# Mamba-2 mixer layer: the carried state's part is added to the diagonal product in PSUM, C times each head's growth on GpSimd, and a new order of the unit

## The chip, the cores and the metric

The kernel runs on one core of one Trainium2 chip. The metric is the device time of one execution in microseconds (us), the median of several runs. A profiled execution is one such run with the hardware profiler on; its "span" goes from the first to the last instruction.

## What is computed

The reference is a layer norm, a Mamba-2 (state space) mixer with a residual, a second layer norm, and a dense layer with a low-rank mixture added, with a residual. Nearly all of the work is the mixer. Sizes: batch 2, sequence 512 in 4 chunks of 128, hidden 512, 128 heads of 64, state 128, 8 groups of 16 heads that share B and C.

```python
L = jnp.exp(_segsum(A_dt))
Y_diag = jnp.einsum('bzlhn,bzshn,bhzls,bzshp->bzlhp', Cc, Bc, L, xch)
states = jnp.einsum('bzlhn,bhzl,bzlhp->bzhpn', Bc, decay_states, xch)
...
Y_off = jnp.einsum('bzlhn,bzhpn,bhzl->bzlhp', Cc, prev, jnp.exp(A_cum))
Y = (Y_diag + Y_off).reshape(b, s, H, P) + hs * D[None, None, :, None]
g = y * jax.nn.silu(gate)
```

`Y_diag` is the part inside a chunk, `Y_off` what the state of the earlier chunks brings, multiplied by `exp(A_cum)`, here called a head's growth. Then follow a norm over each group of 1024 channels and the output projection.

## The kernel before

The instructions of every engine are written out by hand, with semaphores between the engines; nothing is scheduled by a compiler. `mixer` walks over 8 groups (`g`) of 8 units (`j`, running number `k`). A unit is 128 channels, two heads (`PAIR`), for both batches (`b`). Products of weights are made of three products of a high and a low part in fp32r, each with 512 moving columns (I call these the large matmuls); the small ones are fp32 with 128 columns, and each such matmul shows as two records in the profile. In a unit TensorE does:

- `project` (L708) of the next unit's x into `x_bank` and of its gate into `g_bank`, 12 large matmuls for each batch, 48 in all; in units 4 and 5 also the next group's B and C (24 more);
- `out_product` (L766) for four 128-token blocks, 24 large matmuls, c = 0, 1 into `x_bank`, c = 2, 3 into `d_bank`;
- `states` (L718), `diagonal` (L726, into `d_bank`), `carry` (L735) and `turn_hs` (L742, transposes), the small ones. One bank, `turn_bank`, takes the transposes of both batches in turn, and one, `state_bank`, the states and the carried product of both batches in turn, so the four steps for a batch are spread between the large ones.

VectorE reads x out of PSUM with three taps of the convolution (`tap`, L1072), multiplies the transposed x by dt (`to_heads`, L1143), the decay matrix by B·C (`score`, L1098), carries the state over the chunks (`carried_state`, L1106), and makes y in three steps: `carry_part` (L1123) multiplies the carried product in `state_bank` by the growth, `skip` (L1130) adds D·x to the diagonal product, `add_carry` (L1136) adds the two. `y_low_part` (L1092) makes y's low part, `add_outs` (L1160) adds output blocks into `acc`, and `normed_out` (L1171) adds the last group's 8 finished blocks, scaled, into `mixed`: 2, 3 and 3 of them in units 1, 2 and 3 of each group after the first. In units 5 and 6 VectorE has three taps more, for B and C (`bc_tap`, L1082). ScalarE makes the exponentials (`decays`), the silus, y's high part and its square (`finish`), and the weights' high parts (`high_part`). GpSimd multiplies y by the gate (`gated`, L1319), dt·x by the decay (`decayed`, L1325), sums squares (`add_squares`, L1312) and makes low parts of weights (`low_part`, L1306, and L1343). SyncE issues all loads in one queue; `load_grown` (L622) copies each head's growth to 64 partitions.

## Time and profile before

| what | value |
|---|---|
| runs (3) | median 1673.87 us, 1670.74 to 1675.4 |
| the profiled execution | 1673.45 us, span 1671.7 us |
| mean granted clock of TensorE | 0.989 of full speed |
| DMA | 164.56 MB, mean 98 GB/s |

The busy shares of the engines are in the first rows of the section below. A unit is best read as the distance from its first `d_bank` matmul (L731) to the next unit's.

### The profile page before, as it was taken

Reading aid. Unit: us, or ns where it says so; the run is one execution under the profiler, and the core shown is the slowest. Engines: PE = TensorE matmul, PEld = TensorE weight load, DVE = VectorE, ACT = ScalarE, POOL = GpSimd, SP = SyncE. Lnnn points to the kernel's source line nnn. Section 1 sums busy time; section 2 is a strip of 40 time slices with the busy share of each in tenths; the row PEclk is TensorE's granted clock in tenths of the full one; section 3 lists DMA queues with packets and bytes.
Section 4 is the critical chain, followed back from the end, with each engine's and each line's share of the span. In section 5 each row is a group of like instructions: output and inputs, shape, how many; then the busy total and the mean of one; then the engine's idle time right before and its main releaser. Section 6 shows DMA issues by size and latency. Waiting matters only on the chain.

```text
span 1671.7 us, 26883 instructions
## 1 busy us (share of the span) xinstructions
PE 1620.5 (97%) x9616; PEld 1343.2 (80%) x9616; DVE 1361.8 (81%) x1974; ACT 1140.1 (68%) x2002; POOL 838.9 (50%) x543
## 2 busy tenths in 40 slices
PE   7779999999999999999999999999999999999987
PEld 4568888888888888888888888888888888888866
DVE  7567787997889788897879978897888978799756
ACT  5577667776787677766677767776777666877721
POOL 1145545564455545465445644565454654556542
PEclk9989999999999999999999999999999999999988
DMA  5423232323232332332223232323323232233111
GB/s 200 178 96 112 80 109 88 109 83 107 97 98 90 104 102 80 111 97 87 101 91 107 93 107 86 105 82 107 102 76 112 101 97 87 96 101 108 58 41 51
DMA packets 88244, 164.56 MB, mean 98 GB/s; under 512 B 23344, under 2 KB 39728, under 8 KB 87856
## 3 DMA queue, kind: packets, MB, share of 16 engines
q1 hardware_dynamic: 88112, 162.85, 30.0%
q8 instruction: 77, 1.26, 0.3%
q14 instruction: 55, 0.45, 0.1%
HBM read 157.03 MB, written 5.77 MB: 97 GB/s over the span
## 4 chain that ended last, share of the span: by engine, by line
PE 77%; issue 7%; POOL 6%; DVE 5%; ACT 1%; DVEq 0%; POOLq 0%; ACTq 0%
PE g_bank L713 7%; PE g_bank L715 7%; PE g_bank L714 7%; PE x_bank L713 6%; PE x_bank L715 6%; PE d_bank L731 6%; PE x_bank L714 6%; PE state_bank L738 5%; PE state_bank L722 5%; PE turn_bank L745 3%; PE x_bank L772 3%; PE x_bank L770 3%; PE x_bank L771 3%; PE d_bank L772 3%; PE d_bank L770 3%
## 5 line engine op out<-in xcount | busy, mean ns | idle before, releaser
L1323 POOL TENSOR_TENSOR y<-y,gate 128x512 f32<-128x512 f32 x128 | 223.4, 1745 | 457.5 <-DVE y L1140 457.5
L1078 DVE SCALAR_TENSOR_TENSOR hs<-x_bank,cols,hs 128x1022 f32<-128x1022 f32 (+2 forms) x192 | 244.6, 1274 | 85.1 <-ACT hs L940 82.8
L930 ACT ACTIVATE scores<-scores,tables 128x128 f32<-128x128 f32 x1024 | 312.4, 390 | 1.1 <-DMA scores<-sums_dram 1.1
L713 PE MATMUL g_bank<-x_high,w_high 128*128 128x512 f32 x624 | 258.0, 413 | 1.2 <-DVE bc L1156 1.2
L1330 POOL TENSOR_TENSOR xdecay<-xdt,tables 128x384 f32<-128x384 f32 x128 | 146.1, 1141 | 200.6 <-DVE xdt L1150 200.6
L715 PE MATMUL g_bank<-x_high,w_low 128*128 128x512 f32 x624 | 245.6, 394 | 0.0
L714 PE MATMUL g_bank<-x_low,w_high 128*128 128x512 f32 x624 | 243.9, 391 | 0.0
L1309 POOL TENSOR_TENSOR w_low<-raw,w_high 128x512 fp32r<-128x512 f32 x141 | 192.5, 1374 | 91.0 <-ACT w_high L920 91.0
L713 PE MATMUL x_bank<-x_high,w_high 128*128 128x512 f32 x512 | 213.8, 418 | 0.5 <-PEq L146 0.5
L715 PE MATMUL x_bank<-x_high,w_low 128*128 128x512 f32 x512 | 202.0, 395 | 0.0
L714 PE MATMUL x_bank<-x_low,w_high 128*128 128x512 f32 x512 | 200.9, 392 | 0.0
L952 ACT ACTIVATE hs<-hs 128x1024 f32<-128x1024 f32 x64 | 67.9, 1060 | 185.2 <-DVE hs L1078 185.1
L1103 DVE TENSOR_TENSOR scores<-scores,bc 128x1024 f32<-128x1024 f32 x128 | 178.2, 1401 | 8.2 <-ACT scores L933 7.9
L1317 POOL TENSOR_TENSOR square_sum<-square_sum,gate 128x1024 f32<-128x1024 f32 x56 | 167.9, 2998 | 2.2 <-ACT gate L981 2.2
L1169 DVE TENSOR_TENSOR acc<-d_bank,acc 128x512 f32<-128x512 f32 x96 | 65.4, 689 | 99.9 <-PE d_bank L772 99.9
L715 PEld LDWEIGHTS g_bank<-x_high,w_low 128*128 128x128 f32 x624 | 117.5, 188 | 27.3
L933 ACT ACTIVATE scores<-scores 128x1024 f32<-128x1024 f32 x128 | 135.9, 1062 | 2.8
L714 PEld LDWEIGHTS g_bank<-x_low,w_high 128*128 128x128 f32 x624 | 118.2, 189 | 21.2
L713 PEld LDWEIGHTS g_bank<-x_high,w_high 128*128 128x128 f32 x624 | 118.1, 189 | 21.4 <-DVE bc L1156 1.5
L731 PEld LDWEIGHTS d_bank<-scores,xdt 128*64 128x64 f32 x2048 | 110.5, 137 | 24.2 <-issue 22.2
L1117 DVE SCALAR_TENSOR_TENSOR state<-state,chunk_tab,state_bank 128x64 f32<-128x64 f32 x512 | 121.1, 278 | 9.1
L731 PE MATMUL d_bank<-scores,xdt 128*64 128x128 f32 x2048 | 126.2, 276 | 1.7 <-DVE xdt L1150 1.7
(172 smaller groups left out, 3602.6 us busy)
## 6 DMA issues: line engine op xcount, KB each, us to landing
scores<-sums_dram SPq DMA_DIRECT2D x128, 512.0 KB, 4.9
raw<-w_in SPq DMA_DIRECT2D x144, 256.0 KB, 3.0
grown_rows<-grown_dram SPq DMA_DIRECT2D x256, 96.0 KB, 2.7
out_raw<-w_out SPq DMA_DIRECT2D x64, 256.0 KB, 3.2
xt<-x SPq DMA_DIRECT2D x8, 256.0 KB, 5.3
mixed<-x SPq DMA_DIRECT2D x1, 2048.0 KB, 11.7
out<-mixed SPq DMA_DIRECT2D x8, 256.0 KB, 2.0
table_dram<-table SPq DMA_DIRECT2D x2, 768.0 KB, 3.2
```

The costliest lines, as they stand in the source:

```text
L713: pe.matmul(to, w_high[:, slot, k], x_high[:, b, k], start=(k == 0), stop=False)
L714: pe.matmul(to, w_high[:, slot, k], x_low[:, b, k], start=False, stop=False)
L715: mm = pe.matmul(to, w_low[:, slot, k], x_high[:, b, k], start=False, stop=(k == KT - 1))
L731: mm = pe.matmul(d_bank[r * HEAD_DIM:(r + 1) * HEAD_DIM, b, c * P:(c + 1) * P], xdt[:, b, c, r], scores[:, s, b, r, c], start=True, stop=True)
L930: op = s.activation(at, at, ACT.Relu, bias=col[:, r, c:c + 1], scale=-1.0)
L933: s.activation(scores[:, q % 2, b], scores[:, q % 2, b], ACT.Exp, scale=-1.0).then_inc(exp_ready, 1)
L1078: v.scalar_tensor_tensor(out=hs[:, q % 2, :, i:], in0=x_bank[:, :, 0:SEQ - i], scalar=cols[:, q, TAPS - 1 - i:TAPS - i], in1=hs[:, q % 2, ...
L1103: v.tensor_tensor(at, at, bc[:, b].rearrange("p c l -> p (c l)").unsqueeze(1) .to_broadcast([P, PAIR, SEQ]), ALU.mult).then_inc(scores_rea ...
L1309: pool.tensor_tensor(w_low[:, slot], raw[:, slot], w_high[:, slot].bitcast(F32), ALU.subtract)\
L1317: pool.tensor_tensor(square_sum[:], square_sum[:], gate[:, q % 2], ALU.add).then_inc(square_added, 1)
L1323: pool.tensor_tensor(y[:, b], y[:, b], gate[:, q % 2, b], ALU.mult).then_inc(y_ready, 1)
L1330: pool.tensor_tensor(xdecay[:, b], xdt[:, b, 0:LATER], col.unsqueeze(3).to_broadcast([P, LATER, PAIR, HEAD_DIM]), ALU.mult)\
```

## The change

- `carry` no longer writes the bare product into `state_bank`. It multiplies by C times growth, which differs by head, so it is two matmuls of 64 output partitions where there was one of 128, and it accumulates on the diagonal product in `d_bank`. Only `skip` is left to make y, now for each batch.
- `grown_of` on GpSimd multiplies `grown_c` by C in place, 128x768 for each batch. `load_grown` copies both heads' growth to all 128 partitions, twice the bytes, and waits for `carried`.
- Each batch has its own bank (`head_bank`) for transposes and states.
- TensorE's unit is now: outputs c = 2, 3 of the unit before, x for both batches, states and diagonal of both, gate for both, outputs c = 0, 1, (B or C of the next group), carry of both, transposes of both. There are two stretches of 36 large matmuls.
- VectorE, ScalarE and GpSimd are reordered to match.

```diff
     x_bank, g_bank, d_bank, turn_bank, state_bank = banks
     out_bank = [x_bank[:, 0], x_bank[:, 1], d_bank[:, 0], d_bank[:, 1]]
+    head_bank = [turn_bank, state_bank]
...
-        grown = sb("grown_rows", [P, BATCH, LATER, P])
+        grown_c = sb("grown_c", [P, BATCH, PAIR, LATER, P])
...
             def load_grown(k, b):
-                reached(sp, y_sum, BATCH * (k - 1) + b + 1)
+                reached(sp, carried, BATCH * (k - 1) + b + 1)
                 rows = grown_dram[b * ALL + k].rearrange("(r n) -> r n", r=PAIR)
-                for r in range(PAIR):
-                    sp.dma_start(grown[r * HEAD_DIM:(r + 1) * HEAD_DIM, b].rearrange("p c l -> p (c l)"),
-                                 rows[r, P:].partition_broadcast(HEAD_DIM)).then_inc(grown_in[b], 16)
+                sp.dma_start(grown_c[:, b].rearrange("p r c l -> p r (c l)"), rows[:, P:].partition_broadcast(P))\
+                  .then_inc(grown_in[b], 16)
...
                 for c in range(CHUNKS):
                     for r in range(PAIR):
                         mm = pe.matmul(d_bank[r * HEAD_DIM:(r + 1) * HEAD_DIM, b, c * P:(c + 1) * P],
-                                       xdt[:, b, c, r], scores[:, s, b, r, c], start=True, stop=True)
+                                       xdt[:, b, c, r], scores[:, s, b, r, c], start=(c == 0), stop=False)
                 mm.then_inc(diag_done, 1)
...
             def carry(k, b):
+
                 pe.wait_ge(state_ready, BATCH * k + b + 1)
+                pe.wait_ge(grown_c_ready, BATCH * k + b + 1)
                 for c in range(LATER):
-                    mm = pe.matmul(state_bank[:, c * P:(c + 1) * P], state[:, b, c].rearrange("p r d -> p (r d)"),
-                                   c_feat[:, b, (c + 1) * P:(c + 2) * P], start=True, stop=True)
+                    for r in range(PAIR):
+                        mm = pe.matmul(d_bank[r * HEAD_DIM:(r + 1) * HEAD_DIM, b, (c + 1) * P:(c + 2) * P],
+                                       state[:, b, c, r], grown_c[:, b, r, c], start=False, stop=(c == LATER - 1))
                 mm.then_inc(carried, 1)
 
             def turn_hs(k, s, b):
                 pe.wait_ge(hs_ready, k + 1)
+                reached(pe, state_ready, BATCH * (k - 1) + b + 1)
                 for c in range(CHUNKS):
-                    mm = pe.transpose(turn_bank[:, c * P:(c + 1) * P], hs[:, s, b, c * P:(c + 1) * P], ident[:])
+                    mm = pe.transpose(head_bank[b][:, c * P:(c + 1) * P], hs[:, s, b, c * P:(c + 1) * P], ident[:])
                 mm.then_inc(turned, 1)
...
+            def later_outs(j, k):
+
+                for c in (2, 3):
+                    if k < ALL:
+                        pe.wait_ge(y_sum, BATCH * k + c - 1)
+                    else:
+                        pe.wait_ge(added, emptied(k - 1, c))
+                    out_product(j, c)
...
+                    if k > 2:
+                        later_outs(j - 1, k - 1)
+                    if k == ALL + 1:
+                        pe.wait_ge(square_added, (UNITS - 1) * GROUPS)
+                        var_of()
                     if ahead:
                         pe.wait_ge(conv_ready, k + 1)
-                        reached(pe, added, emptied(k - 1, 0))
-                        project(ahead[0], x_at, 0, x_bank[:, 0])
+                        for b in range(BATCH):
+                            reached(pe, added, emptied(k - 1, b))
+                            project(ahead[0], x_at, b, x_bank[:, b])
...
+                            pe.wait_ge(b_tok_ready, g + 1)
+                        for b in range(BATCH):
+                            states(k, b)
                         for b in range(BATCH):
                             reached(pe, added, emptied(k - 1, 2 + b))
                             diagonal(k, s, b)
...
+                        for b in range(BATCH):
+                            project(ahead[0], x_at + 1, b, g_bank[:, b])
+                    if k > 1:
                         pe.wait_ge(y_low_ready, k - j % 2)
                         pe.wait_ge(out_low_ready, k - j % 2)
...
+                    if j in (4, 5) and not last:
+                        pe.wait_ge(gate_ready, BATCH * (k + 2))
+                        for b in range(BATCH):
+                            project(g, (NEXT_B, NEXT_C)[j - 4], b, g_bank[:, b])
+                    if now:
+                        for b in range(BATCH):
+                            carry(k, b)
                     if ahead:
...
+                        for b in range(BATCH):
+                            turn_hs(k + 1, (j + 1) % 2, b)
+                    if j == 0 and g > 0:
+                        pe.wait_ge(square_added, (UNITS - 1) * g)
+                        pe.wait_ge(gate_ready, BATCH * (k + 2))
+                        var_of()
...
                     if ahead:
-                        decays(k + 1, ahead[0], ahead[1], 1)
                         tap0(*ahead)
...
                     if ahead:
+                        decays(k + 1, ahead[0], ahead[1], 0)
                         silu_hs(k + 1, (j + 1) % 2)
...
-                    if second:
-                        decays(k + 2, second[0], second[1], 0)
+                    if ahead:
+                        decays(k + 1, ahead[0], ahead[1], 1)
+                    if j == UNITS:
+                        group_std(GROUPS)
...
-            def skip(q, k):
-                v.wait_ge(diag_done, BATCH * (k + 1))
+            def skip(q, k, b):
+                v.wait_ge(carried, BATCH * k + b + 1)
                 reached(v, squared, k)
-                v.scalar_tensor_tensor(out=y[:], in0=hs[:, q % 2], scalar=d_col[:, q:q + 1], in1=d_bank[:],
-                                       op0=ALU.mult, op1=ALU.add).then_inc(skip_added, 1)
+                v.scalar_tensor_tensor(out=y[:, b], in0=hs[:, q % 2, b], scalar=d_col[:, q:q + 1], in1=d_bank[:, b],
+                                       op0=ALU.mult, op1=ALU.add).then_inc(y_sum, 1)
...
-                    turn_over, takes_bc = j == UNITS - 1 and not last, j in (5, 6) and not last
-                    early = isinstance(g, int) and g == 0
-                    flush = not (early and j < 2)
-
-                    to_heads(g, j, k, 1)
-                    if turn_over:
-                        keep_bc(g + 1)
-                    if takes_bc:
+
+                    for b in range(BATCH):
+                        to_heads(g, j, k, b)
+                    if k > 2:
+                        add_outs(g, j - 1, (2,))
+                    if j in (5, 6) and not last:
                         for i in range(1, TAPS):
                             bc_tap(i, 2 * (g + 1) + j - 5, j - 5)
-                        carried_state(*now, 0)
-                    elif ahead:
-                        score(ahead[0], ahead[1], k + 1, 0)
+                    for b in range(BATCH):
+                        score(g, j, k, b)
+                    if k > 2:
+                        add_outs(g, j - 1, (3,))
+                    if j == UNITS - 1 and not last:
+                        keep_bc(g + 1)
                     if prev:
                         y_low_part(prev[1], prev[2])
-                    if not takes_bc:
-                        carried_state(*now, 0)
-                    if not early:
+                    if j == 1 and g > 0:
+                        group_rstd(g)
+                    if g > 0:
                         for at in {1: (0, 1), 2: (2, 3, 4), 3: (5, 6, 7)}.get(j, ()):
                             normed_out(g, at)
                     if ahead:
-                        tap(1, *ahead)
-                    carry_part(k, 0)
-                    if ahead:
-                        tap(2, *ahead)
-                        tap(3, *ahead)
-                    carried_state(*now, 1)
-                    skip(j, k)
-                    add_carry(k, 0)
-                    if takes_bc:
-                        score(ahead[0], ahead[1], k + 1, 0)
-                    if ahead:
-                        score(ahead[0], ahead[1], k + 1, 1)
-                    carry_part(k, 1)
-                    add_carry(k, 1)
-                    if flush:
+                        for i in range(1, TAPS):
+                            tap(i, *ahead)
+                    for b in range(BATCH):
+                        carried_state(*now, b)
+                    for b in range(BATCH):
+                        skip(j, k, b)
+                    if k > 1:
                         add_outs(g, j, (0, 1))
-                    if ahead:
-                        to_heads(ahead[0], ahead[1], k + 1, 0)
-                    if flush:
-                        add_outs(g, j, (2, 3))
-                    if j == 0 and not early:
-                        group_rstd(g)
...
+            def grown_of(q, k, b):
+                if q == 0:
+                    pool.wait_ge(c_ready, k // UNITS + 1)
+                pool.wait_ge(grown_in[b], 16 * (k + 1))
+                at = grown_c[:, b].rearrange("p r c l -> p r (c l)")
+                pool.tensor_tensor(at, at, c_feat[:, b, P:].unsqueeze(1).to_broadcast([P, PAIR, LATER * P]), ALU.mult)\
+                    .then_inc(grown_c_ready, 1)
+
             def body(g, last):
                 for j in range(UNITS):
                     k = UNITS * g + j
-                    prev, ahead = unit(g, last, j - 1), unit(g, last, j + 1)
+                    prev = unit(g, last, j - 1)
                     splits = splits_of(g, last, j)
-                    decayed(j, k, 1)
-                    if prev:
-                        add_squares(*prev)
+                    for b in range(BATCH):
+                        decayed(j, k, b)
+                    for at in splits[:1]:
+                        low_part(*at)
                     pool.wait_ge(out_high_ready, k + 1)
                     pool.tensor_tensor(out_low[:, j % RING], out_raw[:, j % 2], out_high[:, j % RING].bitcast(F32),
                                        ALU.subtract).then_inc(out_low_ready, 1)
-                    for at in splits[:2]:
+                    if prev:
+                        add_squares(*prev)
+                    for b in range(BATCH):
+                        grown_of(j, k, b)
+                    for at in splits[1:]:
                         low_part(*at)
-                    gated(j, k, 0)
-                    gated(j, k, 1)
-                    if ahead:
-                        decayed(ahead[1], k + 1, 0)
-                    for at in splits[2:]:
-                        low_part(*at)
+                    for b in range(BATCH):
+                        gated(j, k, b)
```

The same in the order of instructions. VectorE, third unit of a group (j = 2), before, from its one `score` to `skip`:

```order
L1103 TENSOR_TENSOR scores<-scores,bc 128x1024
L1094 SCALAR_TENSOR_TENSOR y_low<-y,cols,y_high 128x1024
L1112 COPY state<-state_bank 128x128
L1117 SCALAR_TENSOR_TENSOR state<-state,chunk_tab,state_bank 128x64 x4
L1173 SCALAR_TENSOR_TENSOR mixed<-acc,g_rstd,mixed 128x512 x3
L1078 SCALAR_TENSOR_TENSOR hs<-x_bank,cols,hs 128x2x511
L1128 TENSOR_TENSOR grown_rows<-state_bank,grown_rows 128x384
L1078 SCALAR_TENSOR_TENSOR hs<-x_bank,cols,hs 128x2x510
L1078 SCALAR_TENSOR_TENSOR hs<-x_bank,cols,hs 128x2x509
L1112 COPY state<-state_bank 128x128
L1117 SCALAR_TENSOR_TENSOR state<-state,chunk_tab,state_bank 128x64 x4
L1133 SCALAR_TENSOR_TENSOR y<-hs,cols,d_bank 128x1024
```

and now, from the `to_heads` of both batches:

```order
L1128 TENSOR_TENSOR xdt<-turn_bank,tables 128x512
L1128 TENSOR_TENSOR xdt<-state_bank,tables 128x512
L1148 TENSOR_TENSOR acc<-d_bank,acc 128x512
L1095 TENSOR_TENSOR scores<-scores,bc 128x1024 x2
L1148 TENSOR_TENSOR acc<-d_bank,acc 128x512
L1086 SCALAR_TENSOR_TENSOR y_low<-y,cols,y_high 128x1024
L1152 SCALAR_TENSOR_TENSOR mixed<-acc,g_rstd,mixed 128x512 x3
L1070 SCALAR_TENSOR_TENSOR hs<-x_bank,cols,hs 128x2x511
L1070 SCALAR_TENSOR_TENSOR hs<-x_bank,cols,hs 128x2x510
L1070 SCALAR_TENSOR_TENSOR hs<-x_bank,cols,hs 128x2x509
L1104 COPY state<-turn_bank 128x128
```

Both scores, y_low and the three `normed_out` (`mixed`) now follow each other ahead of the taps (`hs`); before, one score stood here and the other behind `skip`.

GpSimd, the same unit, before, from `decayed`:

```order
L1330 TENSOR_TENSOR xdecay<-xdt,tables 128x384 x2
L1317 TENSOR_TENSOR square_sum<-square_sum,gate 128x1024
L1343 TENSOR_TENSOR out_low<-out_raw,out_high 128x512
L1309 TENSOR_TENSOR w_low<-raw,w_high 128x512 x2
L1323 TENSOR_TENSOR y<-y,gate 128x512 x2
```

and now:

```order
L1294 TENSOR_TENSOR xdecay<-xdt,tables 128x384 x2
L1273 TENSOR_TENSOR w_low<-raw,w_high 128x512
L1316 TENSOR_TENSOR out_low<-out_raw,out_high 128x512
L1281 TENSOR_TENSOR square_sum<-square_sum,gate 128x1024
L1303 TENSOR_TENSOR grown_c<-grown_c,c_feat 128x768 x2
L1273 TENSOR_TENSOR w_low<-raw,w_high 128x512
L1287 TENSOR_TENSOR y<-y,gate 128x512 x2
```

The square sum and the two new products with C stand between the low part of the output weights and the second low part.

VectorE, sixth unit (j = 5), before, behind the taps for B, the first batch's state and the taps:

```order
L1112 COPY state<-state_bank 128x128
L1117 SCALAR_TENSOR_TENSOR state<-state,chunk_tab,state_bank 128x64 x4
L1133 SCALAR_TENSOR_TENSOR y<-hs,cols,d_bank 128x1024
L1140 TENSOR_TENSOR y<-y,grown_rows 128x384
L1103 TENSOR_TENSOR scores<-scores,bc 128x1024 x2
```

and now, from `to_heads` on:

```order
L1128 TENSOR_TENSOR xdt<-turn_bank,tables 128x512
L1128 TENSOR_TENSOR xdt<-state_bank,tables 128x512
L1148 TENSOR_TENSOR acc<-d_bank,acc 128x512
L1079 SCALAR_TENSOR_TENSOR bc_conv<-g_bank,tap_bc,bc_conv 128x2x511
L1079 SCALAR_TENSOR_TENSOR bc_conv<-g_bank,tap_bc,bc_conv 128x2x510
L1079 SCALAR_TENSOR_TENSOR bc_conv<-g_bank,tap_bc,bc_conv 128x2x509
L1095 TENSOR_TENSOR scores<-scores,bc 128x1024 x2
L1148 TENSOR_TENSOR acc<-d_bank,acc 128x512
L1086 SCALAR_TENSOR_TENSOR y_low<-y,cols,y_high 128x1024
```

The scores are now those of the same unit, and stand behind the three taps for B (`bc_conv`).

## Rows read from the trace of the kernel before

**Rows 1.** The page: busy time by engine.
```profile
PE 1620.5 (97%) x9616; PEld 1343.2 (80%) x9616; DVE 1361.8 (81%) x1974; ACT 1140.1 (68%) x2002; POOL 838.9 (50%) x543
```

**Rows 2.** Busy time in stretches, columns in the first line: two middle units, one longer, two first.
```profile
core 0: us, PE busy (x) PEld busy (x) DVE busy (x) ACT busy (x) POOL busy (x), PEclk, DMA share, GB/s
886.45:908.71 22.26, 22.26 (x137) 18.62 (x137) 20.38 (x30) 16.27 (x29) 11.12 (x8) 1.00 0.31 101
908.71:931.48 22.77, 22.70 (x137) 18.47 (x136) 22.40 (x31) 16.26 (x29) 14.53 (x9) 1.00 0.29 99
954.25:981.95 27.70, 27.70 (x161) 23.13 (x161) 18.86 (x29) 18.10 (x31) 14.42 (x11) 1.00 0.28 91
...
81.24:110.91 29.67, 21.35 (x114) 17.01 (x113) 19.39 (x31) 25.61 (x51) 13.90 (x10) 0.83 0.27 85
110.91:131.96 21.05, 18.39 (x114) 15.40 (x113) 15.39 (x23) 16.25 (x29) 11.85 (x8) 0.92 0.30 101
```

**Rows 3.** Timeline of TensorE, start and duration in us: a unit; 36 large matmuls.
```profile
886.45 1.97 PE L731 MATMUL d_bank<-scores,xdt 128*64 128x128 f32 x32
888.35 0.94 PE L738 MATMUL state_bank<-c_feat,state 128*128 128x128 f32 x6
889.04 0.47 PE L713 MATMUL g_bank<-x_high,w_high 128*128 128x512 f32 x1
...
891.89 0.83 PE L722 MATMUL state_bank<-xdecay,b_tok 128*128 128x128 f32 x6
...
966.93 0.48 PE L713 MATMUL g_bank<-x_high,w_high 128*128 128x512 f32 x1
...
975.21 0.60 PE L745 MATMUL turn_bank<-ident,hs 128*128 128x128 f32 x4
```

**Rows 4.** Page, costliest groups: busy us, mean ns of one, idle before.
```profile
L1140 DVE TENSOR_TENSOR y<-y,grown_rows 128x384 f32<-128x384 f32 x128 | 97.2, 759 | 8.9
L920 ACT ACTIVATE w_high<-raw 128x512 fp32r<-128x512 f32 x141 | 87.2, 618 | 10.4 <-PEq L146 10.4
L976 ACT ACTIVATE y_high<-y,cols 128x1024 fp32r<-128x1024 f32 x64 | 73.2, 1144 | 20.8 <-POOL y L1323 20.8
L1128 DVE TENSOR_TENSOR grown_rows<-state_bank,grown_rows 128x384 f32<-128x384 f32 x128 | 70.6, 551 | 7.7 <-PE state_bank L738 6.8
```

**Rows 5.** Timeline of VectorE, five places.
```profile
809.86 3.90 DVE L1087 SCALAR_TENSOR_TENSOR bc_conv<-g_bank,tap_bc,bc_conv 128x1022 f32<-128x1022 f32 x3
...
829.01 1.28 DVE L1169 TENSOR_TENSOR acc<-x_bank,acc 128x512 f32<-128x512 f32 x2
...
834.69 2.36 DVE L1103 TENSOR_TENSOR scores<-scores,bc 128x1024 f32<-128x1024 f32 x1
...
907.50 5.07 DVE L1173 SCALAR_TENSOR_TENSOR mixed<-acc,g_rstd,mixed 128x512 f32<-128x512 f32 x3
...
919.72 1.22 DVE L1103 TENSOR_TENSOR scores<-scores,bc 128x1024 f32<-128x1024 f32 x1
...
1628.69 2.73 DVE L1173 SCALAR_TENSOR_TENSOR mixed<-acc,g_rstd,mixed 128x512 f32<-128x512 f32 x4
```

**Rows 6.** Timeline of GpSimd, two places.
```profile
832.77 0.84 POOL L1330 TENSOR_TENSOR xdecay<-xdt,tables 128x384 f32<-128x384 f32 x1 [0.95 <-DVE xdt L1150]
833.57 2.40 POOL L1317 TENSOR_TENSOR square_sum<-square_sum,gate 128x1024 f32<-128x1024 f32 x1
838.26 1.30 POOL L1343 TENSOR_TENSOR out_low<-out_raw,out_high 128x512 fp32r<-128x512 f32 x1 [2.29 <-ACT out_high L1010]
...
905.25 3.39 POOL L1317 TENSOR_TENSOR square_sum<-square_sum,gate 128x1024 f32<-128x1024 f32 x1
908.61 1.73 POOL L1343 TENSOR_TENSOR out_low<-out_raw,out_high 128x512 fp32r<-128x512 f32 x1
```

**Rows 7.** Timeline of TensorE: a wait at the start, one at the end.
```profile
102.56 0.72 PE L745 MATMUL turn_bank<-ident,hs 128*128 128x128 f32 x4 [3.76 <-DVE xdt L1150]
...
1616.18 3.57 PE L762 MATMUL turn_bank<-mean_col,square_sum 128*128 128x2 f32 x16 [4.17 <-POOL square_sum L1317]
```

156 lines of the change are left out of this document (47 added, 109 removed).

## Prediction

> **What bounds the kernel now.** I read the page first: TensorE is busy for 97% of the span, VectorE 81%, ScalarE 68%, GpSimd 50% [rows 1]. A share over the span could hide waits, so I then read the busy time in stretches from one unit's first `d_bank` matmul to the next [rows 2]. A middle unit takes 22.26 us, all of it TensorE's; a third or fourth unit of a group 22.77, where VectorE is busy for 22.40; a unit with B's or C's projection 27.70. The first two take 29.67 and 21.05 us with 21.35 and 18.39 busy. So TensorE's queue is the bound, and a change can gain by making the same matmuls denser or by removing waits at the two ends. It can lose only if an operand comes late on TensorE, and the engine with least spare time is VectorE.
>
> The sum is made against the profiled execution, 1673.45 us; its span of 1671.7 leaves 1.75 us around it, and the median of the runs is 0.42 us above it, so no correction is needed.
>
> **The change, part by part.**
>
> *Matmuls, per unit.* The large ones are the same 72. Twelve between small ones take 2.85 us (889.04 to 891.89), 36 in one stretch 8.28 (966.93 to 975.21) [rows 3]. Six times 2.85 is 17.1, twice 8.28 is 16.6: 0.5 us less. The new carry is 12 fp32 matmuls of 64 output partitions, 24 records. The diagonal has exactly this form, 32 records in 1.90 us (886.45 to 888.35), so 24 take about 1.45. The old carry is 6 records in 0.69 behind the diagonal [rows 3], and a little less elsewhere, 1.3 for both. That is +0.15, and changing between 64 and 128 output partitions once more adds up to 0.2. Net between -0.35 and +0.05 us per unit; I take -0.1, times 64: **-6 us** (-22 to +3).
>
> *Waits that go.* A third or fourth unit has 0.51 us over the plain one [rows 2], and I allow 0.5 more per group for the turn-over units: 1.5 x 7 = **-11 us**.
>
> *The start.* Units without an output product should take 22.26 - 2 x 2.85 = 16.6 us; the first two take 50.7 together [rows 2], 17.5 over. The waits come from handing one bank from batch to batch, as the 3.76 us of the second transposes for VectorE's xdt [rows 7], and the granted clock is 0.83 and 0.92 there [rows 2]. With a bank per batch I still find 3.5 us (second batch's exponential, first carried state): **-13 us** (-8 to -17).
>
> *The end.* The last output blocks now run while the last y is gated and split, 2.7 us of work in what was idle, and the variance (waiting 4.17 us for the square sum [rows 7]) comes behind an output product: **-4 us** (-1 to -6).
>
> *VectorE's work.* The two 384-column operations per batch go: the addition alone is 0.76 us each [rows 4]. This is costed at nothing, since its spare time is not TensorE's; the cover is TensorE's 22 us per unit. *Growth loads* double to 384 KB per batch, some 25 MB over the run; the DMA share is 0.31 [rows 2], so they too are hidden: the product with C needs them over 10 us after they are issued.
>
> *GpSimd's new products.* 384 columns take 0.84 us alone, 1024 take 2.40, 512 take 1.30 [rows 6]; 768 lie between, 1.8. Twice per unit, 3.6 us. GpSimd is busy for 11 to 14.5 of 22 us [rows 2], so its queue holds that. What it costs is VectorE's time. A VectorE operation that has two SBUF inputs waits for a GpSimd operation that is running: the score at 834.69 ended 1.08 us after the square sum that began at 833.57 (+2.40), taking 2.36 instead of 1.22; three `normed_out` took 5.07 us beside GpSimd, while four took 2.73 without it [rows 5, 6]. That is 1.69 each: GpSimd's 1.3 for a 512-column operation and 0.4 of its own. The two take turns, an operation each. So beside GpSimd each such operation costs the whole of whatever GpSimd has in its queue there.
>
> The Trainium skill says the same as a rule ("SBUF — State Buffer", Who interferes with whom): the later of the two fully blocks until the first finishes. By that rule an operation of 2.3 us blocks for 2.3; if instead a block never exceeded the 1.3 us that this trace shows, the sum would be the first rival's. The turns in rows 5 and 6 agree with the rule, for operations up to 1.3 us.
>
> *Third and fourth unit.* I lay the new order out in time from T, the start of a unit's first stretch. TensorE: 8.3 outputs and x, 3.2 states and diagonal, 5.5 gates, so at **T+17.0** it needs the taps (`out_product` into `x_bank`). VectorE: `skip` may start when the first carry ends, T-1.1; two skips, two adds, two xdt and one add at about 0.62 (1.28 for two [rows 5]) bring it to T+3.2. GpSimd: gates y until T+2.2, then ScalarE makes y's high part (1.14), the square of like length and two copies of 0.62 [rows 4], so GpSimd's row of work starts at T+5.5 and has no gap: low part, output weight's low part, square sum 2.3, 1.8, 1.8. VectorE in turns with it: scores end T+6.0 (0.6 blocked by xdecay), add 6.6, y_low 8.3, first `normed_out` 10.0 (behind the output weight), second 12.7 (behind the square sum), third 15.1 (behind the first product with C); three taps of 3.7 (three such take 3.90 [rows 5]) end at **T+18.9**. TensorE waits 2.0 us. With two `normed_out` (second unit) the taps end by T+17, without any by T+13.5: no wait. Two units, 7 groups: **+28 us**.
>
> *Sixth and seventh unit.* Three taps for B or C stand ahead of the scores, T+3.2 to 7.0. First score: behind the output weight's low part, 9.0. Second: behind the square sum, 12.4; the add that frees `d_bank` 13.0. TensorE wants the second diagonal at T+10.6 and gets it at 13.1, 2.5 us late. Two units, 7 groups: **+35 us**.
>
> Sum: 1673.45 - 6 - 11 - 13 - 4 + 28 + 35 = 1702.5, say **1702 us**. This case's own range is 1685 to 1722.
>
> **The rivals.**
> 1. *Faster: the new waits hardly appear.* If a block costs 1.15 us at most, the taps end at T+17.1 and the second diagonal is 1.3 late: 14 x 1.3 = 18, 1658 us. It also comes out so if GpSimd's row of work starts a few tenths later than I have it, since the first score of the sixth unit misses its turn by 0.3 us only; with no waits at all it is 1640. For it: VectorE loses 1.5 us per unit and more of work. Against: the whole-operation turns of rows 5 and 6.
> 2. *About the same: one of the two places waits, not both.* 1639.5 + 28 = 1667.5 or + 35 = 1674.5.
> 3. *Slower still: the clock.* The second unit has a granted clock of 0.92 over 21.05 us [rows 2]: some 3.4 us at 1.2 instead of 2.4 GHz, 1.7 us lost, behind a wait like the 3.76 us one [rows 7]. If each of 28 waits of 2 us or more did that, +1.7 x 28 = 48: 1750 us. Against it: a group's steady waits here are 0.5 us, so no row shows what 2 us do.
> 4. *The carry is not paired* in the two halves of the output partitions as the diagonal is: 24 records at 0.11 us, +1.3 per unit, 1785 us. The identical form of L731 speaks against it.
>
> **How the numbers follow.** Forecast 0.48, first rival 0.30, second 0.12, third 0.08, fourth 0.02. A measurement tells 0.3% (5 us) from no change. Faster: the first rival, 0.30. Same: most of the second, 0.10. Slower: the rest, 0.60. For eight in ten the range starts inside the first rival, where 18 us of waits and a larger gain at the start still fit, 1645, and ends above the forecast's own range, 1725; the third and fourth rival and the lowest part of the first stay out.
>
> **What would show it.** Right: units three and four at about 24 us, six and seven with 2.5 us of idle TensorE before the diagonal, ended by VectorE's add or score; scores and `normed_out` well over 1.2 and 0.74 us, taking turns with square sum and `grown_c`; a plain unit at 22.1 to 22.3; the first `d_bank` matmul of the third unit some 13 us earlier; carry records like the diagonal's. Wrong: all middle units at about 22.2, or a wait for GpSimd's `grown_c` before the carry, which I place at T+17 against a need at T+19.7.

## The result, and where the 34 microseconds came from

The changed kernel takes **1707.76 us** (median of four runs, 1706.11 to 1709.0) where the kernel before takes 1674.36 (1670.74 to 1675.4): a ratio of 1.020, interval 1.0186 to 1.0214. Forecast were 1702 and "slower", with a range of 1645 to 1725. The profiled span went from 1671.7 to 1707.3 us.

The page of the kernel after, busy time by engine and then the granted clock in 40 slices:

```profile
PE 1622.7 (95%) x10384; PEld 1348.9 (79%) x10384; DVE 1282.8 (75%) x1782; ACT 1151.1 (67%) x2002; POOL 1036.5 (61%) x671
...
PEclk9899999999999999999999999999999999999999
```

Against [rows 1] VectorE has lost 79 us of busy time, though part of what is left is blocking, GpSimd has gained 198, and TensorE's busy time is 2.2 us more with 768 records more. The span is 35.6 us longer, so nearly all of that is time in which TensorE waits. Where it does, the stretches from one first diagonal to the next show. Kernel after, a second, a third, a fourth and a sixth unit of one group, then the first two units of the run:

```profile
core 0: us, PE busy (x) PEld busy (x) DVE busy (x) ACT busy (x) POOL busy (x), PEclk, DMA share, GB/s
905.24:927.53 22.29, 22.29 (x150) 18.70 (x149) 18.21 (x27) 17.54 (x31) 12.64 (x10) 1.00 0.40 119
927.53:951.51 23.98, 22.57 (x150) 18.62 (x149) 22.19 (x29) 16.20 (x30) 16.63 (x11) 1.00 0.36 110
951.51:975.45 23.94, 22.54 (x150) 18.62 (x149) 20.51 (x27) 16.30 (x31) 16.61 (x11) 1.00 0.36 111
1003.18:1033.19 30.01, 27.98 (x174) 23.18 (x173) 22.29 (x28) 18.92 (x33) 18.10 (x12) 1.00 0.36 100
...
84.74:104.07 19.33, 17.37 (x125) 14.18 (x125) 13.86 (x21) 19.21 (x35) 12.51 (x9) 1.00 0.49 144
104.07:120.93 16.86, 16.86 (x125) 14.19 (x125) 14.00 (x20) 16.77 (x30) 14.22 (x10) 1.00 0.52 157
```

Beside [rows 2]: the plain unit has hardly moved (22.26 to 22.29), the third is 23.98 instead of 22.77, the fourth 23.94, a unit with B's or C's work up to 30.0 instead of 27.70, and the first two take 36.2 instead of 50.7. The waits of TensorE name the two places. Kernel after; waiter, releaser, us in total, times, longest:

```profile
PE d_bank L732 <- DVE acc L1148: 29.0, 15, 2.0
PE x_bank L775 <- DVE hs L1070: 19.6, 14, 1.4
```

The first is the second batch's diagonal in the sixth and seventh unit of seven groups, released by the add that VectorE does behind the second score. The second is the first output product in the third and fourth unit, waiting for the taps. Each also costs 0.2 to 0.3 us of restart, so the distances grow by 2.25 and 1.67 us.

The fourth unit of that group, as VectorE (first block) and GpSimd (second) saw it, T = 941.81; start and duration in us. The third unit has the same durations to 0.01 us:

```profile
944.74 2.88 DVE L1095 TENSOR_TENSOR scores<-scores,bc 128x1024 f32<-128x1024 f32 x2
...
948.14 1.70 DVE L1086 SCALAR_TENSOR_TENSOR y_low<-y,cols,y_high 128x1024 fp32r<-128x1024 f32 x1
949.76 6.80 DVE L1152 SCALAR_TENSOR_TENSOR mixed<-acc,g_rstd,mixed 128x512 f32<-128x512 f32 x3
956.49 3.90 DVE L1070 SCALAR_TENSOR_TENSOR hs<-x_bank,cols,hs 128x1022 f32<-128x1022 f32 x3
```
```profile
948.72 2.26 POOL L1316 TENSOR_TENSOR out_low<-out_raw,out_high 128x512 fp32r<-128x512 f32 x1
950.94 2.82 POOL L1281 TENSOR_TENSOR square_sum<-square_sum,gate 128x1024 f32<-128x1024 f32 x1
953.71 4.56 POOL L1303 TENSOR_TENSOR grown_c<-grown_c,c_feat 128x768 f32<-128x768 f32 x2
```

The three `normed_out` take 6.80 us (5.07 in [rows 5]) beside the square sum and the products with C; the taps end at T+18.6 (forecast T+18.9). And the seventh unit, VectorE and GpSimd; the sixth, 30.01 us earlier, has the same durations:

```profile
1026.42 3.90 DVE L1079 SCALAR_TENSOR_TENSOR bc_conv<-g_bank,tap_bc,bc_conv 128x1022 f32<-128x1022 f32 x3
1030.24 5.42 DVE L1095 TENSOR_TENSOR scores<-scores,bc 128x1024 f32<-128x1024 f32 x2
1035.58 0.68 DVE L1148 TENSOR_TENSOR acc<-d_bank,acc 128x512 f32<-128x512 f32 x1
```
```profile
1031.22 3.35 POOL L1281 TENSOR_TENSOR square_sum<-square_sum,gate 128x1024 f32<-128x1024 f32 x1
1034.53 5.60 POOL L1303 TENSOR_TENSOR grown_c<-grown_c,c_feat 128x768 f32<-128x768 f32 x2
```

They take turns: the first score waits for the output weight's low part, the square sum (2.40 us alone [rows 6], 3.35 here) for the first score, and the second score for the square sum: it ends at 1035.6, 1.1 us behind the square sum's end at 1034.6, so its own work of 1.22 us [rows 5] runs only there. One by one the two scores take 2.12 and 3.38 us: the low part holds the first for 0.9 us, the square sum the second for 2.2. In the kernel before, the square sum of such a unit ends 11 us before its scores begin. VectorE and GpSimd of the kernel before, sixth unit:

```profile
991.33 3.45 DVE L1103 TENSOR_TENSOR scores<-scores,bc 128x1024 f32<-128x1024 f32 x2
```
```profile
977.58 2.40 POOL L1317 TENSOR_TENSOR square_sum<-square_sum,gate 128x1024 f32<-128x1024 f32 x1
```

The account of the +35.6 us of span, from the distances of all 64 units: ahead of the first diagonal +3.5; first two units -14.5; the unit distances of the rest without their new waits -6.2 (last less first diagonal, less the first two units: 1460.7 us in the kernel both_moved below against 1466.9 before); taps late 23.4; second diagonal late 31.5; the clock of TensorE, below, 4.7; from the last diagonal to the end -6.8. The two ends are known less well than the middle: in the eight traces of the kernel after and of the variants below that leave no work out and keep TensorE's order, the first diagonal starts at 82.2 to 85.7 us and the stretch from the last one to the end takes 65.4 to 67.3. The kernel before has one trace, with 81.2 and 72.8.

### The profile page after: what moved, and what is told of

The parts are those of the page before. It is cut to its first block, busy times and chain, and to the rows that moved or that the text cites. A ratio compares the mean times of both kernels' runs of the same rounds, so it can differ in the third digit from the quotient of the medians.

```text
span 1707.3 us, 28048 instructions
## 1 busy us (share of the span) xinstructions
PE 1622.7 (95%) x10384; PEld 1348.9 (79%) x10384; DVE 1282.8 (75%) x1782; ACT 1151.1 (67%) x2002; POOL 1036.5 (61%) x671
## 4 chain that ended last, share of the span: by engine, by line
POOL 51%; issue 39%; PE 3%; ACT 2%; DVE 1%; POOLq 0%; DVEq 0%; ACTq 0%
POOL grown_c L1303 15%; POOL w_low L1273 10%; POOL square_sum L1281 7%; POOL y L1287 7%; POOL out_low L1316 7%; POOL xdecay L1294 6%; ACT scores L925 1%; DVE mixed L1152 0%; PE turn_bank L798 0%; PE turn_bank L800 0%; PE turn_bank L799 0%; PE g_bank L756 0%; PE state_bank L800 0%; PE state_bank L798 0%; PE state_bank L799 0%
## 5 line engine op out<-in xcount | busy, mean ns | idle before, releaser
L1287 POOL TENSOR_TENSOR y<-y,gate 128x512 f32<-128x512 f32 x128 | 162.5, 1292 | 391.4 <-DVE y L1118 391.3
L1118 DVE SCALAR_TENSOR_TENSOR y<-hs,cols,d_bank 128x512 f32<-128x512 f32 x128 | 90.2, 745 | 288.6 <-PE d_bank L742 288.6
L1303 POOL TENSOR_TENSOR grown_c<-grown_c,c_feat 128x768 f32<-128x768 f32 x128 | 279.8, 2207 | 0.0
L713 PE MATMUL g_bank<-x_high,w_high 128*128 128x512 f32 x624 | 252.9, 405 | 1.3 <-DVE bc L1135 1.3
L935 ACT ACTIVATE hs<-x_bank,cols 128x1024 f32<-128x1024 f32 x64 | 77.1, 1204 | 213.2 <-PE x_bank L715 156.4
L1095 DVE TENSOR_TENSOR scores<-scores,bc 128x1024 f32<-128x1024 f32 x128 | 212.6, 1699 | 7.3 <-ACT scores L928 7.1
L713 PE MATMUL x_bank<-x_high,w_high 128*128 128x512 f32 x512 | 199.5, 390 | 0.5 <-PEq L146 0.5
L1281 POOL TENSOR_TENSOR square_sum<-square_sum,gate 128x1024 f32<-128x1024 f32 x56 | 161.7, 2888 | 2.2 <-ACT gate L976 2.2
L732 PE MATMUL d_bank<-scores,xdt 128*64 128x128 f32 x2048 | 130.3, 278 | 30.7 <-DVE acc L1148 29.0
```

Of the source, the lines that this page charges most:

```text
L713: pe.matmul(to, w_high[:, slot, k], x_high[:, b, k], start=(k == 0), stop=False)
L732: mm = pe.matmul(d_bank[r * HEAD_DIM:(r + 1) * HEAD_DIM, b, c * P:(c + 1) * P], xdt[:, b, c, r], scores[:, s, b, r, c], start=(c == 0), st ...
L1095: v.tensor_tensor(at, at, bc[:, b].rearrange("p c l -> p (c l)").unsqueeze(1) .to_broadcast([P, PAIR, SEQ]), ALU.mult).then_inc(scores_rea ...
L1281: pool.tensor_tensor(square_sum[:], square_sum[:], gate[:, q % 2], ALU.add).then_inc(square_added, 1)
L1287: pool.tensor_tensor(y[:, b], y[:, b], gate[:, q % 2, b], ALU.mult).then_inc(y_ready, 1)
L1303: pool.tensor_tensor(at, at, c_feat[:, b, P:].unsqueeze(1).to_broadcast([P, PAIR, LATER * P]), ALU.mult)\
```

## The experiments

The expectations count units from 0, so their unit 2 is the third and their unit 5 the sixth; "A" is the theory of the prediction. Line numbers in the rows are of each run's own kernel, which differ by a few. The kernel before took 1674.6 to 1675.5 us (medians) beside these runs.

### Moving VectorE's two blocked pieces

```
# normed_late, VectorE: between y_low_part and the taps
-                    if g > 0:
-                        for at in {1: (0, 1), 2: (2, 3, 4), 3: (5, 6, 7)}.get(j, ()):
-                            normed_out(g, at)
# and put behind carried_state, ahead of skip; add_outs, where it overwrites acc:
                     if j % UNITS in (2, 3):
+                        reached(v, mixed_ready, TB * (g - 1) + CHUNKS * b + c + 1)
# scores_first: bc_tap(1..3) of j = 5, 6 now stand behind the two score(g, j, k, b)
# both_moved: both edits together
```

> The kernel after the change, with VectorE's two or three normed_out updates of units 1, 2 and 3 of a group moved from ahead of the taps to behind the carried states. Theory A (VectorE's updates whose inputs all lie in SBUF take turns with GpSimd's products, so that they stretch wherever GpSimd is busy): the three updates stood beside the square sum and the growth products at 6.80 us; behind the carried states GpSimd has run out of work, so they cost nearer 0.7 to 1.7 us each, and the taps end about 6 us earlier. TensorE's wait ahead of the first outs of units 2 and 3 (1.69 and 1.65 us, in seven groups, 23.4 us together) goes: 1684 us (1680 to 1689); the wait of the diagonal for the scores stays at about 29 us. Theory B (VectorE has too much work in these units, whatever stands beside it): the updates take their 6.8 us at the new place too and make the skip late: no gain, 1705 to 1715. Theory C (the growth transfers of double size are the cause): no change, 1707.

Measured **1684.1 us** (1680.09 to 1685.53). VectorE and GpSimd in the third unit:

```profile
912.56 3.91 DVE L1070 SCALAR_TENSOR_TENSOR hs<-x_bank,cols,hs 128x1022 f32<-128x1022 f32 x3 [1.67 <-ACT hs L935]
...
918.82 2.29 DVE L1153 SCALAR_TENSOR_TENSOR mixed<-acc,g_rstd,mixed 128x512 f32<-128x512 f32 x3
```
```profile
917.92 1.32 POOL L1274 TENSOR_TENSOR w_low<-raw,w_high 128x512 fp32r<-128x512 f32 x1
```

The same three updates take 2.29 us instead of 6.80 where GpSimd has one last low part left; third and fourth unit are 22.29 in all groups, and the diagonal's wait is 28.9 us, no different from the kernel after (29.0). That is what A expected; B and C, which expected no gain, fall here. The taps would be in time behind this move whether or not anything is blocked, since the updates no longer stand ahead of them; what speaks for the turns is the 2.29 us against 6.80.

> The kernel after the change, with the scores of units 5 and 6 put ahead of the three taps of B or C on VectorE. Theory A: the pair of scores then stands beside GpSimd's xdecay and low parts and no longer beside the square sum, and ends 4 us earlier; the diagonal's wait of 2.25 us in two units of seven groups (31.5 us) goes. The taps of B or C end near 12.3 us behind the start of the outs, where TensorE wants their bank at 11.6, and the taps of the next unit end up to 1 us late, so 0 to 1.2 us of each 2.25 come back: 1683 us (1676 to 1695). Theory B (VectorE's amount of work sets these two units): the wait only moves from the diagonal to the next bank, and the gain is under 5 us: 1703 to 1708. Theory C (double growth transfers): no change.

Measured **1673.33 us** (1670.02 to 1674.26). A's direction, and below its range: the whole 31.5 us goes without the small price that was expected, and in this trace the clock falls behind no unit of the steady part, which gives back the 4.7 us too. Sixth unit, VectorE:

```profile
974.49 2.88 DVE L1095 TENSOR_TENSOR scores<-scores,bc 128x1024 f32<-128x1024 f32 x2
977.29 3.90 DVE L1079 SCALAR_TENSOR_TENSOR bc_conv<-g_bank,tap_bc,bc_conv 128x1022 f32<-128x1022 f32 x3
...
981.70 1.49 DVE L1086 SCALAR_TENSOR_TENSOR y_low<-y,cols,y_high 128x1024 fp32r<-128x1024 f32 x1
```

The scores cost 2.88 for two instead of 5.42, the taps of B pass the square sum unhindered, and y_low comes to 1.49 instead of 2.24. VectorE starts the next taps 12.9 us behind its first skip instead of 16.2, so nothing is late.

> Both moves at once: normed_out behind the carried states, and the scores of units 5 and 6 ahead of the taps of B and C. Theory A: the two gains lie in different units and add: 1660 us (1652 to 1672), faster than the kernel before the change (1674). Theory B: no gain over the two alone, 1700 or more. Theory C: 1707.

Measured **1649.3 us** (1648.99 to 1649.86), ratio to before **0.984** (0.9827 to 0.986): 1.6% faster than the kernel before, 3.4% faster than the change. That is below A's range too, as the small price of scores_first did not come. It is what was forecast as the first rival's "no waits at all", 1640, but for 9 us. The gains of the two moves (24 and 34) add to 58. Page:

```profile
PE 1609.9 (98%) x10384; PEld 1346.0 (82%) x10384; DVE 1157.5 (70%) x1782; ACT 1152.5 (70%) x2002; POOL 990.7 (60%) x671
```

VectorE does the same 1782 instructions in 125 us less busy time than in the kernel after.

### GpSimd's side: length, order, and which product

```
# halved_ops, GpSimd
-                pool.tensor_tensor(square_sum[:], square_sum[:], gate[:, q % 2], ALU.add).then_inc(square_added, 1)
+                for b in range(BATCH):
+                    op = pool.tensor_tensor(square_sum[:, b], square_sum[:, b], gate[:, q % 2, b], ALU.add)
+                op.then_inc(square_added, 1)
# and grown_of: one tensor_tensor per head r on grown_c[:, b, r] instead of one for both
```

> The kernel after the change, with GpSimd's square sum cut in two halves of 512 columns and each growth product cut in two of 384, one per head; the work and its place in GpSimd's order are the same. Theory A in its strict form (an update of VectorE waits until the product that GpSimd has begun is through): each of VectorE's updates waits half as long, the two scores of units 5 and 6 take about 4.2 us instead of 5.42, the three normed_out about 5.2 instead of 6.80, and some 25 us come back: 1683 us (1675 to 1690). Rival D (the two engines share the port evenly while both are at work, whatever the length of an instruction): durations and time stay, 1705 to 1710, or rise by GpSimd's cost of three more instructions per unit.

Measured **1666.61 us** (1664.96 to 1668.88). VectorE and GpSimd, sixth unit:

```profile
971.67 4.32 DVE L1095 TENSOR_TENSOR scores<-scores,bc 128x1024 f32<-128x1024 f32 x2
```
```profile
972.64 4.48 POOL L1282 TENSOR_TENSOR square_sum<-square_sum,gate 128x512 f32<-128x512 f32 x2
```

The score pair takes 4.32 us, 4.2 expected, at the same work: a block lasts as long as the other engine's instruction, and sharing by halves (D) is refuted. The time fell by 41 us where 25 were expected, because a wait is a difference: the mean `normed_out` fell from 2.04 to 1.58 us, which is enough to bring the taps of the third and fourth unit in time (22.29 to 22.35), so 23.1 of those 23.4 us went; the diagonal's wait fell to 13.7 us in total, which takes 15 us off the distances; and behind the shorter waits the clock did not fall, another 4.7.

```
# growth_tiny: grown_of multiplies grown_c[:, b] [:, :, 0:1] by c_feat[:, b, P:P + 1] only
# squares_tiny: add_squares adds gate[:, q % 2, :, 0:1] to square_sum[:, :, 0:1] only
# both_tiny: both
# growth_late, GpSimd's body: all the work kept, order changed
-                    for b in range(BATCH):
-                        grown_of(j, k, b)
                     for at in splits[1:]:
                         low_part(*at)
+                    for b in range(BATCH):
+                        grown_of(j, k, b)
```

> The kernel after the change, with each growth product of GpSimd cut to the first column of each head (128x2 in place of 128x768); the transfers, waits and semaphores stay, so the carry is made with growth that lacks C in all other columns. Theory A: the three normed_out of units 2 and 3 keep only the square sum beside them, take about 4 us instead of 6.80, and the taps are in time: the waits of units 2 and 3 (23.4 us) go; the second score of units 5 and 6 stands beside the square sum, not beside the growth products, and its wait (31.5 us) stays: 1684 us (1680 to 1690), with the d_bank wait at 28 to 32 us. Theory C' (the growth products themselves are the whole price of the change): both waits go, 1650 to 1655. Theory C (the transfers of double size): 1707.

Measured **1697.1 us** (1689.98 to 1698.44), where 1684 was expected. The parts are as A had them: third and fourth unit 22.33 to 22.39, the diagonal's wait 29.0 us in total, as it was. GpSimd beside the scores of the sixth unit (5.41 us the pair) shows why the product with C is innocent there:

```profile
987.27 3.34 POOL L1281 TENSOR_TENSOR square_sum<-square_sum,gate 128x1024 f32<-128x1024 f32 x1
990.57 1.32 POOL L1303 TENSOR_TENSOR grown_c<-grown_c,c_feat 128x2 f32<-128x2 f32 x2
```

The excess is elsewhere: seven of the 14 long waits have a unit of 31.6 or 27.9 us behind them, where the others have 30.0 and 26.35. This is the clock, see longer_wait. Seven times 1.6 us is 11, of which the expectation held the 4.7 of the kernel after; the other 6.5 make 1690, and the profiled run took 1689.98. It is the fastest of the four. The other three, without a trace, have a mean granted clock of 0.981 to 0.983 against its 0.987, which fits more such falls.

> The kernel after the change, with GpSimd's sum of the squares cut to the first column of each batch (128x2 in place of 128x1024), so that the group norm is made from the first unit's squares; the growth products stay whole and follow at once. Theory A: in units 5 and 6 the second score meets a growth product of 1.7 us in place of the square sum of 2.4: of the wait of 2.25 us about 1 goes, 14 us over the kernel; in units 2 and 3 the normed_out meet the same growth products about 2 us earlier, and 0.7 to 1.6 of the 1.67 us go, 10 to 23 us: 1678 us (1668 to 1690). Theory C' (the growth products alone): no gain, 1705 or more.

Measured **1648.72 us** (1646.87 to 1649.12), nearly all of both waits gone (0.1 us stays in the sixth and in the seventh unit), with the products with C whole. 1678 had been expected. VectorE and GpSimd, sixth unit:

```profile
965.67 3.26 DVE L1095 TENSOR_TENSOR scores<-scores,bc 128x1024 f32<-128x1024 f32 x2
```
```profile
966.65 1.19 POOL L1281 TENSOR_TENSOR square_sum<-square_sum,gate 128x2 f32<-128x2 f32 x1
967.80 5.62 POOL L1304 TENSOR_TENSOR grown_c<-grown_c,c_feat 128x768 f32<-128x768 f32 x2
```

I had let the second score wait for the first product with C instead of the square sum. It was its turn before that: the score began about when the tiny sum ended, and the product waited for the score (5.62 us for two products here, 3.67 us for two in the third unit of normed_late). Who has to wait is decided by who comes first, at every instruction anew.

> The kernel after the change, with both of GpSimd's new neighbours cut to a column: the growth products and the sum of the squares; VectorE's order is that of the change. Theory A: nothing long of GpSimd's stands beside the scores and normed_out: both kinds of wait go and the kernel takes what it takes with both moves of VectorE, 1649 us (1645 to 1656). Theory B (VectorE's amount of work in these units): 1700 or more. Theory C (transfers): 1707.

Measured **1649.34 us** (1648.63 to 1651.34): as expected, the same as both_moved, with VectorE's order untouched. So neither VectorE's amount of work nor the doubled growth transfers, which are all still there, cost anything.

> The kernel after the change, with GpSimd's two growth products put behind the second weight tile's low part (1.28 us) instead of ahead of it; VectorE's order is the change's. Theory A: in units 2 and 3 the last normed_out meets the low part in place of a growth product of 1.7 us and more, the three take about 5.9 us instead of 6.80, and half of the two waits (1.67 us each, seven groups) goes: 1696 us (1688 to 1702); units 5 and 6 keep their wait of 2.25 us. Theory B (VectorE's amount of work alone): 1707.

Measured **1704.94 us** (1701.94 to 1705.45), 1696 expected. The three updates took 6.24 us, not 5.9, so third and fourth unit are 23.4: 1.1 us of the 1.67 stays, a gain of 7.9; and the clock took 3.2 back, behind 5 of the 14 long waits instead of 3. The median is only 2.8 us below that of the kernel after and outside the range expected, so it is the unit distances, not the total, that show the gain. The direction held, the size was off.

### What a longer wait does to the clock

```
# longer_wait, VectorE, j = 5, 6: y_low_part ahead of the scores
+                    if prev and j in (5, 6):
+                        y_low_part(prev[1], prev[2])
                     for b in range(BATCH):
                         score(g, j, k, b)
```

> The kernel after the change, with the low half of y of units 5 and 6 put ahead of the scores on VectorE (behind the taps of B or C), so that TensorE's wait for the second score grows. Theory A: the low half costs 1.3 to 2.5 us there and the diagonal's wait of 2.25 us becomes 3.6 to 4.8: 14 places by 2 us, +28, 1735 us (1725 to 1742) if nothing else follows. Theory E (a wait of TensorE of 2 us and more lets the granted clock fall for the matmuls behind it; in the kernel after it fell behind 3 of the 14 waits of 2.25 us, in growth_tiny behind 7, at 1.6 us each, never behind the waits of 1.2 us of halved_ops): it now falls behind nearly each of the 14, 17 to 30 us more, 1757 us (1748 to 1772).

Measured **1772.76 us** (1772.62 to 1775.53), above both. TensorE's idle time before the diagonals is 36.6 + 30.1 us, against 30.7 in the kernel after, and every group's unit behind them is long. Per group the three distances come to 94.3 us (30.30, 35.44, 28.6), 14.8 over both_moved's 79.5; 9.4 of that is idle time; the other 5.4 are restarts (some 0.2 us for each of four waits) and the clock, an estimated 2.3 us for each of the two units. Stretches of longer_wait around one such wait, then of the kernel after around one of its three:

```profile
1036.00:1041.50 5.50, 1.63 (x21) 1.22 (x20) 5.50 (x2) 5.45 (x12) 5.50 (x3) 0.99 0.19 40
1041.50:1045.00 3.50, 2.66 (x18) 2.23 (x19) 3.43 (x5) 0.18 (x1) 3.09 (x2) 0.50 0.00 0
1045.00:1048.50 3.50, 3.50 (x11) 2.72 (x10) 3.36 (x11) 2.00 (x2) 0.00 (x0) 0.55 0.84 287
1048.50:1051.50 3.00, 3.00 (x15) 2.48 (x14) 0.04 (x1) 0.60 (x1) 0.00 (x0) 1.00 0.36 102
```
```profile
396.00:401.30 5.30, 3.28 (x37) 2.55 (x37) 5.30 (x4) 5.25 (x12) 5.30 (x3) 0.96 0.12 22
401.30:404.30 3.00, 3.00 (x9) 2.34 (x8) 2.93 (x4) 0.07 (x1) 3.00 (x2) 0.51 0.00 0
404.30:407.50 3.20, 3.20 (x16) 2.63 (x15) 3.06 (x11) 2.27 (x3) 0.01 (x1) 1.00 0.62 218
```

PEclk, the column behind POOL's, is 0.50 and 0.51, the 1.2 GHz level, and 1.00 again behind it. With 2.0 us of idle time it came in 3 of 14 places of the kernel after, 7 of growth_tiny, 5 of growth_late and 1 of normed_late; with the longer idle time in all 14; with the 0.9 us of halved_ops in none. It fell behind none of the 28 waits of at most 1.4 us for the taps in the traces of the kernel after and of scores_first either. Theory E holds in kind, and its price was set too low for the longer wait (1.6 taken, about 2.3 measured), as was the wait itself.

### The matmuls: the merged stretch and the pairing, and what is left

```
# stretch_split, on both_moved, TensorE (conditions left out; the wait of a group's first unit for b_tok_ready
# moves ahead of both batches)
-                        for b in range(BATCH): project(ahead[0], x_at, b, x_bank[:, b])
-                        for b in range(BATCH): states(k, b)
+                        for b in range(BATCH):
+                            project(ahead[0], x_at, b, x_bank[:, b])
+                            states(k, b)
# carry_unpaired, on both_moved, TensorE
-                for c in range(LATER):
-                    for r in range(PAIR):
+                for r in range(PAIR):
+                    for c in range(LATER):
# moved_halved: both_moved and halved_ops together
```

> The kernel with both of VectorE's moves (both_moved, in which TensorE waits in no unit past the second), with one of the change's merged stretches split again on TensorE: projection of batch 0, states of batch 0, projection of batch 1, states of batch 1, in place of both projections and then both states. By the rows of before (12 large 2.856 and 2.946, six states 0.584 each) the four pieces take 6.97 us, merged they take 6.87 (5.44 + 0.67 + 0.76): +0.10 us in 62 units, 1655 us (1651 to 1659) against 1649.3. [...]

Measured **1655.14 us** (1654.91 to 1656.41), +5.8, as expected: a plain unit went from 22.29 to 22.36 (4.3 us in 62 units), the first two units take 1.8 us more. Merging one pair of large stretches is worth 0.07 us per unit. The change merges six stretches into two, four such merges, so 0.28 us by this estimate, and its carry of 24 records takes 0.19 us more than the old 12 (1.46 against 0.69 + 0.58). That leaves -0.09 where the plain unit shows +0.03; 0.12 us per unit isn't accounted for.

> Both of VectorE's moves, and the carry's six matmuls of a batch given one head after the other (three chunks of head 0, then three of head 1) instead of the two heads in turn. If two neighbours that write to different halves of the output partitions run beside each other (the rival of the prediction in which the carry is not paired), the 24 records lose most of that: from 1.46 us to 2.3 or 2.6 us per unit, 64 times, 1649.3 + 54 to 73: 1712 us (1700 to 1725). If the pace of 0.061 us is that of a matmul with 64 output partitions alone, no change: 1649.

Measured **1666.47 us** (1665.97 to 1669.04), +17. The carry of one unit, first in both_moved, then unpaired:

```profile
1029.26 1.53 PE L742 MATMUL d_bank<-grown_c,state 128*64 128x128 f32 x24
```
```profile
499.25 1.80 PE L742 MATMUL d_bank<-grown_c,state 128*64 128x128 f32 x24
```

Taking the heads in turn saves 0.27 us, no more. Paired, a record takes 0.061 us, unpaired 0.072; the old carry, with 128 output partitions, 0.115 [rows 3]. So most of the pace belongs to the form with 64 output partitions, paired or not. Neither of my two prices (nothing, or 0.9 us and more) was right.

> Both of VectorE's moves and GpSimd's halved instructions together. In both_moved TensorE waits for VectorE in no unit of the steady part, so shorter instructions of GpSimd have nothing left to free: 1649 us (1646 to 1653), the same as both_moved. If a part of the blocks still sat on TensorE's path unseen: 1640 or less.

Measured **1649.42 us** (1648.6 to 1650.57): nothing left to free. TensorE's queue itself is the bound of both_moved.

## Why the prediction was right

*What bounds the kernel.* Right: TensorE's queue, with VectorE the engine whose lateness counts. A plain unit is 22.29 us of TensorE's work.

*Matmuls, -6, and old waits, -11.* Together 17 forecast, 6.2 measured: the one part of the sum that was clearly mis-sized. The matmuls gave nothing: a plain unit was forecast at 22.16 and takes 22.29, 0.03 more than before and not 0.1 less. The old waits and the turn-over units gave about 8: 0.48 us in each third and fourth unit, and in the turn-over units 0.56 less in the seventh against 0.36 more in the eighth. The prediction's bounds of -0.35 to +0.05 us per unit don't follow from its own terms either: -0.5, +0.15 and up to +0.2 give -0.35 to -0.15, and neither the -0.1 that it took nor the measured +0.03 lies in there. The saving in the large stretches is there (24 large in 5.44 us), but the small matmuls behind a large stretch take longer than in the kernel before: the six states 0.67 and 0.76 us, not 0.58, and the prediction had left them as they were. stretch_split puts the net worth of one merge at 0.07 us, where 2.85 against 8.28 / 3 had given 0.09 and the entry into the small ones was counted as free.

*The start, -13.* Measured -11.0: -14.5 in the first two units and +3.5 ahead of the first diagonal. Of the 14.5 us 9.0 are idle time of TensorE and 5.5 busy time, as the granted clock there is 1.00 in place of 0.83 and 0.92 [rows 2]. That it is the bank per batch that does this is argued: no run takes the banks apart from the new order. The +3.5 are no larger than the scatter between the eight traces of the new order (3.5 us); all eight lie above the one trace of before, but how much of it the change costs is not shown.

*The end, -4.* Measured -6.8, and between -5.5 and -7.4 with the eight traces; no run takes its causes apart.

*VectorE's work and the growth loads at nothing.* Right: both_tiny, with all loads and all of VectorE's work, is as fast as both_moved.

*Third and fourth unit, +28.* Measured 23.4: 1.67 us each instead of 2.0. normed_late takes the wait away by moving the updates, growth_tiny and squares_tiny each by shortening one of the instructions that block them. They are over the limit by so little that either one is enough.

*Sixth and seventh unit, +35.* Measured 31.5, and 4.7 for the clock, which the sum did not have in it; that the two make 36.2 is luck. The blocks are those of the output weight's low part (0.9 us) and of the square sum (2.2 us), which the kernel before had too; without the second nearly the whole wait is gone (squares_tiny). The new products have no part in it (growth_tiny leaves it whole). It is the new order that brings the second score to the square sum and to TensorE's need at the same time. The prediction had exactly this row of turns, but gave the heading "GpSimd's new products" to both costs; only the first belongs there.

*The turns.* The second score of the sixth unit waits 2.2 us for the square sum, and halving the sum takes 1.1 us off the pair. So the first rival, a block of 1.15 us at most, is refuted. The Trainium skill ("SBUF — State Buffer", Who interferes with whom) has it as a rule that the later of the two is fully blocked; the trace agrees, now for an instruction of 2.4 us. The same section of the Trainium skill says that the order of issue decides who blocks. squares_tiny agrees: there the second score is ahead of the first product with C, takes its 1.21 us unblocked, and the product takes 2.81 us instead of 1.86.

*The rivals.* The clock rival was priced at 1750 and given 0.08. Of its 28 waits only 14 were of 2 us, and behind three of these the clock fell, 4.7 us: it was a part of the result, not another result. The rival of an unpaired carry was priced at 1785; it would have been 1707.76 + 17, 1725.

*The total.* The mechanism was right at both places. That the total came within 6 us of the forecast is in part luck. The sum was too low by 10.8 us (matmuls and old waits), 4.7 (clock) and 2.0 (start), and too high by 4.6 and 3.5 (the two new waits) and 2.8 (end).

## What to carry to other kernels

Before moving an operation of VectorE that has two SBUF inputs, look at what GpSimd runs at the new time: it costs the rest of GpSimd's current instruction on top of its own. Put such operations where GpSimd is idle, let those with an input in PSUM run beside its long ones, and halve the long ones where they can't be avoided; the two moves here turned a 2.0% loss into a 1.6% gain. And a wait is a difference of two times. In the third unit the last of the three updates became 0.55 us shorter in growth_late, and the wait as much; it became 1.6 us shorter in growth_tiny, and nearly the whole wait of 1.67 us went. Neither changed the wait of the sixth unit, whose blocker is another instruction.
